# Two attention stages of a two-layer kernel: outputs two pairs of heads late, and steps written out without a loop

## What is computed

```
# first layer: 16 heads, DK = DV = 64, a causal recurrence over t
G    = G    + k_t (k_t . C_QV)
S_K  = S_K  + k_t k_t^T
C_QV = C_QV + q_t v_t^T
o_t  = q_t . (S_K C_QV - G)          # out = concat(o) @ W_o

# second layer: 16 heads of 8, relative positions clipped to +-64
scores = (q . k + q . pe_k[dist]) * hd**-0.5
p      = softmax(scores)
ctx    = p v + sum_j p_ij pe_v[dist_ij]   # out = ctx @ W_out + b_out
```

## Time and profile before

| | us |
|---|---|
| median of 3 runs | 1857.75 (1856.51 to 1859.38) |
| the profiled execution | 1857.91 |
| its span, first to last instruction | 1856.3 |
| PE busy in the span | 1681.9 (91%) |
| weight loads (PEld) | 1301.4 (70%) |
| DVE | 921.0 (50%) |
| ACT | 763.5 (41%) |
| POOL | 296.7 (16%) |

### The profile page before, as it was taken

The page is one execution under the profiler, slowest core; times in us unless marked ns, Lnnn a source line. Parts: engine busy times, 40 slices in busy tenths (PEclk is TensorE's granted clock), DMA queues, the critical chain, the costliest instruction groups (busy, mean ns, idle before and its releaser), DMA issues. The chain is left out here.

```text
span 1856.3 us, 38958 instructions
## 1 busy us (share of the span) xinstructions
PE 1681.9 (91%) x13272; PEld 1301.4 (70%) x13272; DVE 921.0 (50%) x3198; ACT 763.5 (41%) x2111; POOL 296.7 (16%) x375
## 2 busy tenths in 40 slices
PE   3698999999999999999789999859989989898896
PEld 3466878888888888888655566537777777677775
DVE  4322554545454545454522222247667667666674
ACT  1232222222222222222222322257767677776773
POOL 1001020101010101010060000012223222232222
PEclk9899999999999999999889999979999999999998
DMA  1200930000000000000043332167877777777785
GB/s 46 61 0 8 88 84 7 7 7 8 4 10 1 11 0 11 0 11 1 7 142 103 102 102 92 51 201 225 234 210 216 208 225 217 208 208 202 222 224 156
DMA packets 230822, 181.82 MB, mean 98 GB/s; under 512 B 82591, under 2 KB 219641, under 8 KB 230640
## 3 DMA queue, kind: packets, MB, share of 16 engines
q1 hardware_dynamic: 225266, 167.14, 34.2%
q0 software_dynamic: 5376, 12.44, 2.2%
HBM read 103.60 MB, written 75.78 MB: 97 GB/s over the span
## 5 line engine op out<-in xcount | busy, mean ns | idle before, releaser
L757 DVE TENSOR_TENSOR a0MT<-a0ps_M,mask 128x384 f32<-128x384 f32 x256 | 142.6, 558 | 258.0 <-PE a0ps_M L606 258.0
L1574 DVE CUSTOM_DVE_ANT_0 a1Pm<-a1ps_S,a1Sb 128x256 f32<-128x256 f32 x512 | 196.0, 420 | 147.2 <-issue 143.4
L1512 ACT ACTIVATE a1Pm<-a1Pm,a1nmx 128x256 f32<-128x256 f32 x512 | 254.5, 502 | 0.2
L701 ACT ACTIVATE a0qk<-a0ps_qk 128x512 f32<-128x512 f32 x128 | 76.4, 597 | 423.6 <-PE a0ps_qk L582 384.1
L1507 ACT ACTIVATE a1Rt<-a1ps_R 128x384 f32<-128x384 f32 x264 | 128.9, 488 | 174.3 <-PE a1ps_R L1382 162.5
L1401 PE MATMUL a1ps_T<-ident,a1Pm 128*128 128x128 f32 x1024 | 163.5, 284 | 0.0
L604 PE MATMUL a0ps_M<-a0AT 128*128 128x256 f32 x512 | 154.0, 383 | 0.0
L752 DVE TENSOR_TENSOR a0AT<-a0ps_A,mask 128x384 f32<-128x384 f32 x256 | 130.8, 552 | 38.4 <-PE a0ps_A L591 36.4
L1143 DVE TENSOR_TENSOR f1hid<-f1ge,f1ps_b 128x512 f32<-128x512 f32 x80 | 55.0, 688 | 191.0 <-PE f1ps_b L1076 182.4
L582 PE MATMUL a0ps_qk<-xnT_all,a0w_in 128*128 (+1 forms) x512 | 145.6, 407 | 1.4 <-PEq L310 1.4
L1391 PE MATMUL a1ps_S<-a1stk 72*128 72x256 bf16 x512 | 104.5, 287 | 23.2 <-issue 23.2
(11 more groups left out here) (240 smaller groups left out, 3061.1 us busy)
## 6 DMA issues: line engine op xcount, KB each, us to landing
skew<-a1Rt SPq DMA_DIRECT2D x132, 384.0 KB, 3.6
a1Sb<-skew SPq DMA_DIRECT2D x131, 384.0 KB, 4.8
a1stk<-parts SPq DMA_DIRECT2D x51, 192.0 KB
a1stk<-parts SPq DMA_DIRECT2D x153, 64.0 KB
parts<-a1prt SPq DMA_DIRECT2D x18, 384.0 KB, 4.7
f1w<-in_L_ffn_w_kernel SPq DMA_DIRECT2D x16, 344.0 KB
f1w<-in_L_ffn_w_kernel SPq DMA_DIRECT2D x16, 320.0 KB
f1wo<-in_L_ffn_wo_kernel SPq DMA_DIRECT2D x16, 320.0 KB
```

Source lines behind the costliest of these rows:

```text
L757: nc.vector.tensor_tensor(MT[h][:, :], ps_M[h][:, 0:HB], mask[:, :], ALU.mult).then_inc(M_ready, 1)
L1512: nc.scalar.activation(Pm[:, place(h), :], Pm[:, place(h), :], ACT.Exp, bias=nmx[it][:, h:h + 1], scale=-1.0, accum_out=den[it][:, h:h + 1 ...
L1574: nc.vector.tensor_tensor_reduce(out=Pm[:, place(h), :], in0=ps_S[hp % 2][:, n, :], in1=bias_of(it, hp, n), scale=-1.0, scalar=3.0e38, op0 ...
```

## The change

In the first attention the outputs of pair p - 2 are computed directly behind the scores of pair p, ahead of `project_qk`, instead of the outputs of pair p - 1 ahead of `values`. For that `vv` and `MT` get a second buffer. `project_out` on PE and `add_y` on DVE move from p = 1 to p = 2, keep_o on ACT moves ahead of keep_qk, `second_choice` stays at p = 2 and now stands ahead of `add_y`. `values` gains a wait for the eviction of the values before, `squares` one for the mask of the squares before, and `positions` one for `y_added`. In the second attention `steps` is a plain loop of the program that writes it: all 32 steps stand in the code one after the other, with constants as semaphore values. `tiles_behind` is written so that it gives the same numbers as before.

```diff
-        vv = m.sb("a0v", [P, 2, P])
+        vv = [m.sb(f"a0v{i}", [P, 2, P]) for i in range(2)]
-        MT = [m.sb(f"a0MT{i}", [P, HB]) for i in range(2)]
+        MT = [[m.sb(f"a0MT{i}{h}", [P, HB]) for h in range(2)] for i in range(2)]
...
                 def values(b, p, bb):
                     pe.wait_ge(xb_ready, b + 1)
+                    if p > 0 or not isinstance(b, int) or b > 0:
+                        pe.wait_ge(v_ready, b * PAIRS + p)
...
                 def squares(b, p):
                     for h in range(2):
                         pe.wait_ge(A_ready, (b * PAIRS + p) * 2 + h + 1)
+                        if p > 0 or not isinstance(b, int) or b > 0:
+                            pe.wait_ge(M_ready, (b * PAIRS + p - 1) * 2 + h + 1)
...
                 def positions(g, k):
                     if k == 0:
+                        pe.wait_ge(y_added, B if isinstance(g, int) and g == NG - 1 else 2 * g + 3)
                         pe.wait_ge(gate_step, g * GSTEPS + GSTEPS)
...
                 def batch(b, bb, behind, g, gating):
                     for p in range(PAIRS):
                         scores(b, p)
+                        if behind or p > 1:
+                            outputs(b * PAIRS + p - 2, p % 2)
                         if p < PAIRS - 1:
                             project_qk(b, p + 1)
...
-                        if behind and p == 1:
+                        if behind and p == 2:
                             project_out(b - 1)
...
-                        if behind or p > 0:
-                            outputs(b * PAIRS + p - 1)
                         values(b, p, bb)
                         squares(b, p)
...
-                outputs(B * PAIRS - 1)
+                outputs(B * PAIRS - 2, 0)
+                outputs(B * PAIRS - 1, 1)
...
                     for p in range(PAIRS):
                         if behind and p == 4:
                             root(b - 1)
+                        if p > 1:
+                            keep_o(n + p - 2, p - 2, b)
+                        elif behind:
+                            keep_o(n + p - 2, PAIRS + p - 2, b - 1)
                         if p < PAIRS - 1 or not isinstance(b, int) or b < LAST:
                             keep_qk(n + p + 1)
                         if behind and p == 6:
                             keep_xT(b - 1, 1 - bb)
-                        if p > 0:
-                            keep_o(n + p - 1, p - 1, b)
-                        elif behind:
-                            keep_o(n - 1, PAIRS - 1, b - 1)
-                        keep_v(n + p)
+                        keep_v(n + p, p % 2)
...
                         if p == 1:
-                            if behind:
-                                add_y(b - 1)
                             if bb == 1 and gating:
                                 first_choice(g, 1)
-                        if p == 2 and bb == 1 and gating:
-                            second_choice(g)
+                        if p == 2:
+                            if bb == 1 and gating:
+                                second_choice(g)
+                            if behind:
+                                add_y(b - 1)
...
         def steps(eng, step):
-            for i in range(4):
-                step(0, i)
-            with eng.Fori(1, B // 2) as r:
+            for r in range(B // 2):
                 for i in range(4):
                     step(r, i)
...
         def tiles_behind(r, i):
-            return 2 if not isinstance(r, int) else i
+            return min(2, r * 4 + i)
```

More of the change, by code:

```diff
@@ L607, in squares, with outputs @@
                                          start=False, stop=True).then_inc(M_done, 1)
-                def outputs(n):
+                def outputs(n, i):
                     pe.wait_ge(o_ready, n + 1)
@@ L615, in outputs @@
                         pe.wait_ge(M_ready, n * 2 + h + 1)
-                        nc.tensor.matmul(ps_o[r, 0:T], vv[:, 0, r], MT[h][:, 0:T], start=True, stop=False)
+                        nc.tensor.matmul(ps_o[r, 0:T], vv[i][:, 0, r], MT[i][h][:, 0:T], start=True, stop=False)
                     for h, r in enumerate(rows):
-                        ins = nc.tensor.matmul(ps_o[r, P:T], vv[:, 1, r], MT[h][:, T:HB], start=False, stop=True)
+                        ins = nc.tensor.matmul(ps_o[r, P:T], vv[i][:, 1, r], MT[i][h][:, T:HB], start=False, stop=True)
                     ins.then_inc(o_done, 1)
@@ L701, in keep_qk, with keep_v @@
                     nc.scalar.activation(qk[:, :, :], ps_qk[:, :, :], ACT.Copy).then_inc(qk_ready, 1)
-                def keep_v(n):
+                def keep_v(n, i):
                     act.wait_ge(v_done, n + 1)
-                    nc.scalar.activation(vv[:, :, :], ps_v[:, :, :], ACT.Copy).then_inc(v_ready, 1)
+                    nc.scalar.activation(vv[i][:, :, :], ps_v[:, :, :], ACT.Copy).then_inc(v_ready, 1)
                 def keep_o(n, p, b):
@@ L730, in batch @@
                             keep_xT(b - 1, 1 - bb)
-                        if p > 0:
-                            keep_o(n + p - 1, p - 1, b)
-                        elif behind:
-                            keep_o(n - 1, PAIRS - 1, b - 1)
-                        keep_v(n + p)
+                        keep_v(n + p, p % 2)
                 keep_qk(0)
                 groups(act, batch)
+                keep_o(B * PAIRS - 2, PAIRS - 2, LAST)
                 keep_o(B * PAIRS - 1, PAIRS - 1, LAST)
@@ L752, in mask_A, with mask_M @@
                         nc.vector.tensor_tensor(AT[h][:, :], ps_A[h][:, 0:HB], mask[:, :], ALU.mult).then_inc(A_ready, 1)
-                def mask_M(n):
+                def mask_M(n, i):
                     for h in range(2):
                         v.wait_ge(M_done, n * 2 + h + 1)
-                        nc.vector.tensor_tensor(MT[h][:, :], ps_M[h][:, 0:HB], mask[:, :], ALU.mult).then_inc(M_ready, 1)
+                        nc.vector.tensor_tensor(MT[i][h][:, :], ps_M[h][:, 0:HB], mask[:, :], ALU.mult).then_inc(M_ready, 1)
                 def add_y(b):
@@ L903, in batch @@
                         if p == 1:
+                            if bb == 1 and gating:
+                                first_choice(g, 1)
+                        if p == 2:
+                            if bb == 1 and gating:
+                                second_choice(g)
                             if behind:
                                 add_y(b - 1)
-                            if bb == 1 and gating:
-                                first_choice(g, 1)
-                        if p == 2 and bb == 1 and gating:
-                            second_choice(g)
                         if p == 3 and behind:
@@ L923, in batch @@
                             sums(g, 1)
-                        mask_M(b * PAIRS + p)
+                        mask_M(b * PAIRS + p, p % 2)
                 nc.vector.memset(zeros[:, :, :], 0.0).then_inc(zero_ready, 1)
```

## The result

The changed kernel takes **1800.85 us** (median of four runs, 1797.68 to 1806.95) against 1857.89 for the kernel before in the same set: ratio 0.9697, 95% interval 0.9666 to 0.9728. A second set of five runs gave 1796.63 (1794.73 to 1805.02), ratio 0.9683 (0.9660 to 0.9707). The profiled execution took 1797.99 us, span 1796.4. Forecast were 1795.6, with 1785 to 1812.

What follows compares the result with a forecast made beforehand. It took PE (TensorE) as the bound: density of matmuls in the first attention, idle at loop branches in the second. 24.8 + 4.4 + 33.1 = 62.3 us off 1857.91 gave 1795.6, range 1785 to 1812 for 8 in 10.

Steps and rivals of the forecast that it cites:

- First attention, 24.8 us: First attention's pairs: the new order has three changes of array shape instead of four, 0.197 us in each of 126 pairs.
- rival 1: First attention: 64-row scores directly ahead of 64-column outputs cost a full change, nothing gained there, 1820 us; chance 0.10.
- Start and end, 0: First attention's ends: pair 1 loses its outputs (-0.8), the tail gets a second group and an eviction (+0.7): 0.
- The collision, 4.4 us: First attention, pairs 12 and 13: `dif` gets through before GpSimd's 8.81 us operation, `normalise` is caught; loss 2.3 instead of 6.67.
- Second attention, 33.1 us: Second attention unrolled: 23.2 us of PE's branch idle, 7.0 of slow steps behind branches, 2.9 from constant waits.
- 0.21 less; for the 14 steps of these two kinds 2.9 us: Second attention: waits become constants, as unrolled steps 2 and 3 took 0.21 us less than in the loop; bounds 0 and 5.9.
- 2.4 in as the share of a slow transfer: Second attention: 2.4 of the 9.4 us surplus not idle at the branch is left in, counted as no gain.
- the forecast's own case: Whole kernel: the summed terms hold, 1795.6 us, with bounds from 1786 to 1803; chance 0.68.
- Rival 2: First attention's loop outgrows what the sequencer keeps; four back-edges cost 13 us, 1809 us; chance 0.07.
- Rival 5: Second attention: straight-line code fetched block by block while DMA engines are busy, some 51 blocks, +204 us, 2000; chance 0.02.
- rival 3: Second attention without its rests is held by transfers or ScalarE and gives back half, 1812 us; chance 0.10.
- rival 4: Second attention: unrolling does not help since PE fetches late elsewhere, the 33.1 us stay, 1829 us; chance 0.03.

Runs made afterwards that it cites:

- Run 4: The changed kernel with the outputs of pair p - 2 put back between q/k and values, still two pairs late; 1823.07 us, ratio 0.9825.
- run 1: The changed kernel once more, nothing edited; median 1796.63 us.
- run 2: The kernel before with only the second attention's steps written out, first attention as it was; 1823.04 us, ratio 0.981.
- run 3: The kernel before with only the first attention's outputs moved, second attention's loop as it was; 1845.10 us, ratio 0.9933.
- run 7: The kernel before with filler instructions at the start of PE's, DVE's and ACT's lists, moving its loops along them; 1880.67 us, ratio 1.0126.
- run 5: The changed kernel with the second attention written out on PE alone, the other four engines in the loop; 1836.76 us, ratio 0.9894.
- run 9: The changed kernel with each round of four steps from r = 1 on in a loop of one trip; median 1802.30 us, ratio 0.9701.

## Why the prediction was right, and where not

**First attention, 24.8 us:** right to the hundredth in a plain pair, 4.923 for 5.120 us. Run 4 shows that the place of the outputs is the cause, and rival 1 (the new meeting costs a full change) is out. The sum over the pairs was 3 us too high, though. "Times 126 pairs" took all for plain ones, and the 28 with `route` or `positions` between q/k and values gained 0.10 each: values' start, 0.11 ahead of them, stayed. Pairs 2 to 126, the collision set aside, gave 21.8 us and not 24.6.

**Start and end, 0:** pairs 0 and 1 took 1.3 us less (pair 1: 5.31 to 4.12), and from the last scores to the first step it took 1.3 more.

**The collision, 4.4 us:** 5.05 measured (6.67 lost before, 1.62 after; pair 13 6.5 instead of the 7.3 forecast). The step failed where it said "`dif` at 243.8, through before 245.04": true of `dif`, but the last operation of `moments` starts only 0.2 us before the table's in the changed kernel's first profile, and in two profiles of seven the gain was a loss of 1.4 us instead (8.0 lost in pairs 12 and 13). A margin of tenths beside transfers of 55 us is a chance, and I gave it as a certainty.

**Second attention, 33.1 us:** 37.2 measured (35.0 to 35.5 in runs 1, 2 and 4). The mis-sized term is "0.21 less; for the 14 steps of these two kinds 2.9 us": all four kinds gained, 0.20 and 0.15 by turns, 4.7 in 27 steps. Another 1.4 came back of the "2.4 in as the share of a slow transfer" (479.35 against 13 x 17.97 + 14 x 17.48 = 478.3). The rest of the 27 steps is the loop's fourth step, taken as 18.19 where others of its kind took 18.12. Four steps take 70.9 instead of 71.3.

Its mechanism was half of the truth. "PE idles 23.2 us in six pieces for it. Unrolled, there is no branch" is true of a change that unrolls every engine. As an account of what the loop cost it is wrong: DVE and ACT had their own late code under PE's. Take away PE's branch alone, by place (runs 3 and 7) or by writing PE out (run 5), and the stage gets 7 to 10 us slower. The 4.3 us of PE were cover for a stall of DVE, 4.8 us in run 3, that starts about a microsecond later and, uncovered, costs more. The sum of this stage came out because the visible wait happened to stand for all of them.

**The total, 62.3 forecast and 59.9 measured,** is closer than its terms. The pairs gave 3.0 us less, the collision 0.7 and the second attention 4.1 more, and the first scores started 4.3 later, which no term foresaw. That these nearly cancel is luck. The lower end of the forecast's own case, 1786, is also off: its terms (2.3, 3.0 and 2.4 us) end nearer to 1788.

**Rival 2** argued from length: "a round of 1329 branches in 0.21 us and one of about 1545 in 4.27, so a limit lies between". The first attention's loop did keep its 0.21 us (its body grew from 1408 to 1459 instructions), but there is no such limit; the same body does both (run 7). Rival 5, straight code late per block: 77 packets in PE's list against 41 in the third run, so some 9,000 instructions more, and no wait of PE for issue in the 27 steps. **Rivals 3 and 4:** the DMA share rose from 0.76 to 0.81 and PE's waits for transfers and ScalarE's evictions rose from 6.7 to 10.9 us in 27 steps, yet the steps take the 17.48 and 17.97 us that the two written-out ones took before; nothing was given back.

## What to carry to other kernels

Where the shape of TensorE's array changes within a repeated sequence, count the changes (0.2 us each here, 0.1 where another short piece stands in the gap) and look for an order with fewer; a result used one repeat later can be enough to allow it. A sequencer loop's price is the late code of all its engines at once: the trace shows best the one that the others lie beneath. Written out alone, PE made this stage 7 us slower than it was in the kernel before and DVE made it 17 faster, while all together gained 37. So look at every engine's idle for issue behind the branch, and expect the price to move when instructions are added anywhere ahead of the loop.

## What was not expected of the hardware

- A loop of 1667 instructions on PE branched in 4.27 or in 0.21 us by where it lay in the list. Edits in the first attention moved it, and with that changed a stage they do not touch by 9 us.
- In the last microseconds before the first attention TensorE's clock takes one of two courses, whatever the kernel. Busy time from 175 to 182 us, of the kernel before and of the second attention alone, which are the same program up to there:

```profile
175.00:182.00 7.00, 4.96 (x32) 3.74 (x30) 1.60 (x2) 0.60 (x1) 1.89 (x3) 0.95 0.00 1
```

```profile
175.00:182.00 7.00, 5.71 (x22) 4.56 (x20) 0.69 (x1) 0.00 (x0) 0.00 (x0) 0.50 0.00 0
```

  At 0.50 (1.2 of 2.4 GHz) the first scores start between 184.0 and 186.2 us (five profiles, the changed kernel's first among them), otherwise between 181.3 and 181.9 (seven). Between two profiles of the changed kernel that is 4.4 us. The collision of run 9 goes with it: of the profiles that could show it, all four early ones escape, and two of the three late ones are caught. What chooses the course is open.
- With that, a slow transfer of `a1stk` (5.3 us with the half clock behind it) and the collision (6.4) there are three things in the traces that can make up the changed kernel's spread of 10 us from run to run. The kernel before spreads as widely: over eleven runs from 1852.4 to 1859.8, and over nine others from 1852.7 to 1864.4. Its three runs at first had only seemed steadier.
